# Half of the shared expert's down products, taken from the stretch before the routed rounds to the final sums, in a one-core mixture-of-experts tower

## The reference

```python
logits = xt @ gate_w.T                                   # 15 routed experts
topk_w, topk_idx = jax.lax.top_k(softmax(logits), 3)     # 3 per token
comb = zeros((T, 15)).at[arange(T)[:, None], topk_idx].add(topk_w / sum(topk_w))
...
a = gelu(g) * xh * geglu_mult                            # routed, inner width 256
y = einsum('etd,te->td', a @ fc2_w + fc2_b, comb)
hs = xt @ s_fc1_w.T + s_fc1_b                            # shared expert, inner width 512
xs, gs = hs[..., :512], hs[..., 512:]
ys = (gelu(gs) * xs * s_geglu_mult) @ s_fc2_w.T + s_fc2_b
out = layernorm(h + y + ys)
```

## Time and profile before

| | |
|---|---|
| median of 3 runs | 215.7 us (215.48 to 215.84) |
| the profiled execution's own time | 215.09 us |
| its span in the profile | 213.3 us |
| PE busy | 202.4 us (95%) |
| granted TensorE clock, mean | 0.999 |

### The profile page before, as it was taken

How to read it: one execution, slowest core, us unless ns; L and a number is a source line. 1 busy time by engine, 2 the same in 40 slices (tenths; PEclk the granted TensorE clock), 3 DMA queues, 4 the chain that set the end, 5 groups by cost and what they waited for, 6 DMA issues and landing times.

```text
span 213.3 us, 4443 instructions
## 1 busy us (share of the span) xinstructions
PE 202.4 (95%) x1566; PEld 127.4 (60%) x1566; DVE 112.6 (53%) x313; ACT 94.6 (44%) x219; POOL 120.8 (57%) x148
## 2 busy tenths in 40 slices
PE   8999899989998899989999999999999999998992
PEld 4776577678786675756877773444445554454530
DVE  5685597848873444275599743723434332231044
ACT  2004635578868372553438664233323343224033
POOL 0040089759979857949999376207755662337100
PEclk9999999999999999999999999999999999999999
DMA  6999999940000399941032033118985321112572
GB/s 209 396 413 351 397 417 421 418 173 0 6 3 0 104 365 383 419 111 49 2 101 49 16 105 101 37 35 314 365 323 205 93 81 52 49 49 83 154 279 92
DMA packets 13918, 38.52 MB, mean 181 GB/s; under 512 B 2697, under 2 KB 4682, under 8 KB 13898
## 3 DMA queue, kind: packets, MB, share of 16 engines
q1 hardware_dynamic: 11882, 32.74, 40.9%
q0 software_dynamic: 2016, 5.51, 8.5%
HBM read 29.37 MB, written 4.16 MB: 157 GB/s over the span
## 4 chain that ended last, share of the span: by engine, by line
PE 83%; DVE 8%; DMA 4%; ACT 1%; issue 1%; POOL 1%; SPq 0%; POOLq 0%; DVEq 0%; ACTq 0%
PE ps L381 72%; PE ps L1858 3%; DMA wres<-y_dram 3%; PE ps L1668 2%; PE ps L1898 2%; PE ps L1681 2%; DMA y_dram<-ln_mem,dest_i 1%; PE ps L1600 1%; DVE embed_sb L1326 1%; POOL y_dram L664 1%; DVE ln_mem L1038 1%; DVE nw_i L1022 1%; DVE nw L1028 1%; DVE nw L1027 1%; DVE ln_rs L1006 1%
## 5 line engine op out<-in xcount | busy, mean ns | idle before, releaser
L381 PE MATMUL ps<-wres,cT 128*64 (+1 forms) x360 | 63.1, 469 | 0.6 <-DVE cT L1410 0.6
L381 PEld LDWEIGHTS ps<-wres,cT 128*64 128x64 f32 (+1 forms) x360 | 25.3, 131 | 28.4 <-issue 21.3
L664 POOL DMA_INDIRECT y_dram<-ln_mem,dest_i x21 | 20.6, 983 | 26.7 <-ACT ln_mem L871 23.4
L424 POOL TENSOR_TENSOR wres<-wres,fac_mem 128x512 f32<-128x512 f32 x22 | 27.2, 1270 | 2.9 <-DVE ln_rs L1029 2.9
L655 POOL DMA_INDIRECT embed_sb<-x_dram,gather_i x21 | 20.4, 969 | 12.9 <-PE ps L1858 4.9
L1403 DVE TENSOR_TENSOR fac_mem<-ps,h 128x256 f32<-128x256 f32 x21 | 8.9, 423 | 24.0 <-ACT h L865 24.0
L865 ACT ACTIVATE h<-ps 128x256 f32<-128x256 f32 x21 | 8.0, 383 | 28.5 <-PE ps L381 28.5
L381 PE MATMUL ps<-h,stage 128*128 128x296 f32 x64 | 17.9, 418 | 0.0
L1410 DVE COPY cT<-ps 128x256 f32<-128x256 f32 x21 | 8.8, 424 | 16.3 <-PE ps L381 14.6
L871 ACT ACTIVATE ln_mem<-ps 128x256 f32<-128x256 f32 x21 | 8.0, 383 | 16.4 <-PE ps L381 16.4
L381 PEld LDWEIGHTS ps<-h,stage 128*128 128x128 f32 x64 | 11.8, 190 | 3.8 <-issue 0.4
(11 more groups left out here) (212 smaller groups left out, 385.4 us busy)
## 6 DMA issues: line engine op xcount, KB each, us to landing
wres<-experts SPq DMA_DIRECT2D x15, 768.0 KB, 12.1
fac_mem<-experts SPq DMA_DIRECT2D x11, 256.0 KB, 8.2
wres<-ut SPq DMA_DIRECT2D x3, 768.0 KB, 8.8
embed_sb<-embed SPq DMA_DIRECT2D x5, 416.0 KB, 5.8
stage<-shared SPq DMA_DIRECT2D x2, 771.0 KB, 15.4
wres<-y_dram SPq DMA_DIRECT2D x3, 512.0 KB, 4.6
stage<-wres SPq DMA_DIRECT2D x2, 512.0 KB, 3.5
f1v<-fc_v SPq DMA_DIRECT2D x1, 512.0 KB
```

What stands on the lines that cost most here:

```text
L381: return nc.tensor.matmul(o, w, x, start=start, stop=stop)
L424: nc.gpsimd.tensor_tensor(w1(e, c), w1(e, c), row, ALU.subtract).then_inc(less_done, 1)
L664: pool.indirect_dma_start(out=y_dram[:, :], out_offset=bass.IndirectOffsetOnAxis(ap=dest_i[:, column(i):column(i) + 1], axis=0), in_=ys[:, ...
```

## The change

The down products of the second shared expert (`e` = 1) are no longer made in the units. Their gated inputs stay in SBUF for all tokens (`a_late`, in parts of `h1` and `pair_mem` that are free by then), and they are made at the very end as tokens by features, straight into the sum banks, in place of the two fillers of each tile. `a_sh` shrinks to two blocks, `slot_table` moves from unit 6 to unit 7, the first two `tile_transposed` stand ahead of both `lower_expert`, and one weight copy (`copy_w2[1]`) goes to `h3` instead of `stage`, whose shared weights must now live to the end. `add_input` waits for two down products a half instead of four. DMAs are the same in number, size and order.

```diff
-        a_sh = xn_mem[:, 0:4 * HT].rearrange("p (u t) -> p u t", u=4)
+        a_sh = xn_mem[:, 0:FC * HT].rearrange("p (u t) -> p u t", u=FC)
+        a_late = (h1_mem[:, 2 * F:2 * F + T], pair_mem[:, 2 * TOPK * TT * E:2 * TOPK * TT * E + T])
...
-        copy_w2 = [stage_mem[:, W1C:WC], stage_mem[:, WC + W1C:2 * WC], pt_mem[:, NXG * D + W1C:NXG * D + WC],
+        copy_w2 = [stage_mem[:, W1C:WC], h3_mem[:, W2C:2 * W2C], pt_mem[:, NXG * D + W1C:NXG * D + WC],
...
-                if k >= 4:
-                    dve.wait_ge(y_mm, k - 3)
+                if e == 0 and n == 1:
+                    dve.wait_ge(y_mm, j + 1)
                 nc.vector.scalar_tensor_tensor(
-                    a_sh[:, u], ps[:, 5 + 2 * j, 0:HT], stage[:, e, WC + FC + j:WC + FC + j + 1], gel[:, j],
+                    a_sh[:, j] if e == 0 else a_late[j][:, n * HT:(n + 1) * HT], ps[:, 5 + 2 * j, 0:HT], stage[:, e, WC + FC + j:WC + FC + j + 1], gel[:, j],
...
-                    dve.wait_ge(y_mm, 2 * FC * NS - 4 * (1 - n))
+                    dve.wait_ge(y_mm, FC * (n + 1))
...
-            def down(k, u, e, n):
-
-                j = u % 2
-                pe.wait_ge(t1_done, k + 1)
-                if k % 4 == 0:
+            def down(n, j):
+
+                pe.wait_ge(t1_done, 4 * n + j + 1)
+                if j == 0:
                     pe.wait_ge(scaled, FC * NS)
                 for c in range(DC):
-                    last = mm(ps[:, 2 * n + c, 0:HT], stage[:, e, W1C + j * D + c * P:W1C + j * D + (c + 1) * P],
-                              a_sh[:, u], k % 4 == 0, k % 4 == 3)
+                    last = mm(ps[:, 2 * n + c, 0:HT], stage[:, 0, W1C + j * D + c * P:W1C + j * D + (c + 1) * P],
+                              a_sh[:, j], j == 0, j == FC - 1)
...
-                if k == 6:
+                if k == 7:
                     slot_table()
...
-                if k == 6:
-                    pe.wait_ge(idx_done, 1)
-                    pe.wait_ge(tab_out, 2)
-                    pe.wait_ge(xr_out, 3)
...
-                if k >= 2:
-                    down(k - 2, (u + 2) % 4, (k - 2) // FC % NS, (k - 2) // (NS * FC))
+                if k in (2, 3):
+                    down(0, j)
...
-            down(6, 2, 1, 1)
+            pe.wait_ge(xr_out, 3)
+            pe.wait_ge(idx_done, 1)
+            pe.wait_ge(tab_out, 2)
+            for j in range(FC):
+                down(1, j)
...
+            for i in range(2):
+                tile_transposed(i)
             pe.wait_ge(own_done, 1)
             for i in range(2):
                 lower_expert(i)
-                tile_transposed(i)
-            down(7, 3, 1, 1)
...
-                keep_clock(2, 2)
+                for j in range(FC):
+                    mm(o, a_late[j][:, t * P:t * P + rows], stage[:, 1, W1C + j * D:W1C + (j + 1) * D], False, False)
```

## The result

The changed kernel takes **217.19 us** (median of 7 runs, 216.53 to 218.39), the kernel before 215.56 us (median of 7, 215.42 to 215.99). The ratio is **1.0061 (95% interval 1.0033 to 1.0088)**: 0.6% slower. Two more comparisons of the same pair gave 1.0063 (1.0039 to 1.0088) and 1.0053 (1.0024 to 1.0082), with medians of 216.97 and 216.86 us. The forecast was 215.7 us, no change. Ratios leave out slow executions, those more than 1.5% above the fastest of the same kernel (one of 29 of the changed kernel, at 237.53 us).

The account below looks back on a forecast made before the run. PE's work was taken to bound both the hand-over to the routed tiles and the end; on the median's scale, 215.7 - 2.40 (head) + 2.42 (tail) = 215.7 us, no change, with a range of 214.9 to 216.9 us.

Parts of the forecast that it names:

- The head up to the second transposition: Hand-over from shared units to routed tiles: slot table ends at 119.65 us, second gather lands at 124.86, second transposition near 124.91.
- The new wait: In the hand-over to the routed tiles: PE stands about 1.0 us before the second tile's transposition, until its gather lands.
- the last one of the head: Second transposition to first routed matmul: two loads and five ISAs at 0.10 us each, start at 125.66, head gains 2.40 us.
- rival D: Between second transposition and first routed tile: PE's sequencer cannot read ahead, register loads paid in full, up to 217.1 us; chance 0.20.
- The row of a 0.8 us gap: Longest issue gap before a routed tile's weight load, taken per register load for the upper bound: 2.1 us with ISAs.
- The tail: Last routed tile to the end: late products add 2.92 us for five tiles, 0.50 absorbed by slack, 2.4 us given back.
- rival F: In the head: PE's new 1 us stall drops the clock to 1.2 GHz, 2 us and more on top, from 217.7; chance 0.03.
- The scale: Whole kernel: the profiled execution lies 0.6 us below the median, so 215.1 us becomes 215.7 us on the median's scale.
- B: Cheap loads: in the head they hide behind the transposition, late products cost the lower figure, 214.9 us; chance 0.18.
- C: In the tail: late products are hidden because PE waits for the reads anyhow, 213.3 us; chance 0.05.
- E: In the head: second tile's gather lands 1 us later than 124.86, everything moves by 1 us, 216.7 us; chance 0.07.
- G: In the head: slot table comes later than 119.65, head gain below 1 us, time over 217 us; chance 0.05.

## Why the prediction was wrong

**The head up to the second transposition was right.** Unit 6, the table, the second gather and the second transposition start within 0.1 us of the forecast, counted from unit 4. The new wait was smaller than forecast: PE stands 0.67 us instead of about 1.0, because the work ahead of it ended later.

**The step that failed** is the last one of the head, in its words "I take all seven at those 0.10 us, as the nearest row: 0.7 us beside the transpositions". From the second transposition to the first routed matmul it was 1.83 us instead of 0.75; without the 0.05 us of step that the forecast added, 1.78 instead of 0.70. The head gained 1.37 us instead of 2.40. The mechanism was there as rival D, with the right reason ("cannot read ahead"), and the measured value lies inside the bounds given, 0.22 and 2.1 us. The row chosen was the price of one ISA instruction; a register load is no ISA instruction, so "nearest" was wrong. The row of a 0.8 us gap, which I used as the far end only, was the nearer one: 0.57 and 0.86 us were measured. The forecast's "No row here times one by itself" is not so: the trace of the kernel before times both loads, 484 and 307 ns, and their next instructions, 165 and 156 ns (shown above). From the first load's start to the end of the second's last instruction that is 1.6 us; what was left to judge was only whether it would be hidden or paid. The Trainium skill's figure ("DMA: Bandwidth & Descriptors", "Latency and other measured facts"), a floor of about 600 ns for each `tensor_load`, gave a gain of 1.4 us and 216.7 us. That came near for another reason: the traces do not bear the floor out, since a load takes 0.31 or 0.49 us on PE here, and only with the instructions behind it does it come to 0.66 or 0.85. The page says nothing of what decides here, whether PE stands at a wait ahead of the load.

**The tail was right**: 2.52 us measured, 2.42 forecast; 3.0 us of work (2.92), 0.5 of slack.

**The clock, rival F, was given 0.03 and stays open.** In one trace, of the version without the late products, the clock fell right behind the stall and cost 1.6 us. In the changed kernel's own three traces it did not fall while PE worked, and the trace sum of 1.15 us, without any clock, already gives the measured ratios, which make 1.1 to 1.4 us. Six of its 29 executions, with mean clocks of 0.984 and 0.985, may be of this kind. I had judged the rival by a stretch in which PE had 1.01 us of work in 1.49; here it had 0.44 us in 2.6. The Trainium skill, "TensorE: Matmul & The Clock Gate", "Part 1: The HAM clock gate", has activity release the clock and idleness take it back; the one stretch shown above agrees.

**The scale.** The forecast was put on the median by adding 0.6 us. That was right: the profiled start was early, and the median with more runs is 215.8.

**B, C, E and G** fell: loads are not cheap behind a wait, the tail is bound by PE, the gather came on time, and so did the slot table. The mechanism was rival D's, at a price between its own upper one and the forecast's. With the one term put right, 215.7 + 1.08 = 216.8 us: inside the stated range, as are the third comparison's 216.86 us, while the first two medians, 217.19 and 216.97, lie 0.3 and 0.1 us above it.

## What to carry to other kernels

Where PE will stand at a semaphore, the register loads behind that wait are paid in full: put them ahead of the wait, or leave work between. The sequencer's own rows in the trace show how long they take and whether they ran ahead. Work moved out of a busy stretch only brings what the next waits leave of it; ask for each microsecond removed what is late next, and leave just enough work there to fill the waits (with the loads ahead, half of the move brought 1.4 and 2.1 us in two comparisons, the whole one 0.7; with the loads behind, the whole one cost 1.1 to 1.4). And work moved to where fillers stand is hidden only to the amount by which the engine waited in spite of them.

## What the runs showed of the hardware

Of the two register loads in the head, the first takes 0.48 to 0.49 us on PE and the second 0.31, with their other instructions 0.85 and 0.66 us (all 21 of the kernel before: 0.30 to 1.02, median 0.31). Behind a wait at which PE stood, they began only when the wait was over and delayed the first routed matmul by 0.86 and 0.57 us; where PE had 2.6 us of work from their start on, they delayed nothing. With 0.44 us of work in some 2.6 us on PE, the granted clock was at 1.2 GHz from 128.1 to 131.5 us in one trace, with PE busy throughout, and stayed at 2.4 GHz in three traces of the changed kernel with the same stall. One indirect scatter among the last took 4.2 to 4.4 us to land instead of 2.4, and which one it was differed between traces. PE can stand 0.9 to 1.9 us for issue alone in one comparison and not in another, with the same code. The start of an execution varies with nothing edited there: in fourteen traces unit 4 began between 112.58 and 114.66 us, and the first product, held by the first input load, between 4.13 and 4.77.
